# A two-layer batched kernel: another order for batch 0, adapter sums turned by VectorE, and the last batch's parts finished one behind the other

## Chip, cores and metric

One core of one Trainium2 chip. The metric is the device time in microseconds of one execution.

## The reference, cut to what matters

```python
# B, S, D = 8, 256, 1024; rank 16, 32 adapters
sign = (2 * mask - 1)                          # mask[b] is 1024 x 1024, int32
x = x + (x @ W0.T + b0 + (x @ sign) * coeff[b])    # layer 1
A, Bw = lora_A_w[ids[b]], lora_B_w[ids[b]]
x = x + (x @ W1.T + b1 + (x @ A.T) @ Bw.T)         # layer 2
```

Everything is float32. Each factor is split into a high part in the matmul's reduced format (fp32r) and a low part, the rest; three of the four products are summed.

## The kernel before

Layer 1 of a batch is folded into one matrix: W = W0.T + I + coeff x (2 mask - 1). It is made and used in 8 chunks of 128 output columns, so the kernel has 64 chunks n (b = n // 8, c = n % 8). For a chunk VectorE makes W from the mask (`make_w`, L589), ScalarE its high part (`chunk_hi`, L421), VectorE the low part (`chunk_lo`, L596). TensorE multiplies by x (`layer1`, L756 and L758: for each of 8 k one product of 512 columns, x high and low side by side, and one of 256). ScalarE adds the bias and VectorE adds the two halves to y (`half_y` L447, `make_y` L603), then y is split (`y_parts_hi` L454, `y_parts_lo` L607). y is stored transposed, so it serves as the stationary operand of layer 2.

Layer 2 adds, for chunk c, y's chunk times 1024 columns of W1.T + I and 16 columns of adapter A into six PSUM parts (two halves st of the rows, three parts j of the columns; `layer2`, L800 to L802, three products each of some 344 columns). In batch 0 it is four parts of 512 columns (`first_layer2`, L778 to L780) and the adapter has a product of its own (`adapter_h`, L766). After a batch's last chunk the 16 adapter columns h must be turned and multiplied by adapter B and the bias: ScalarE copies them to SBUF (`move_h`, L469), TensorE transposes them (`turn_h`, L811), ScalarE and VectorE split them into `ht` (`h_parts_hi` L476 and L478, `h_parts_lo` L617), and one product per part finishes it (`finish`, L829; batch 0: L820). ScalarE and VectorE move the parts to `zst` in turn (L489, L629), and SP stores them (`store_z`, L286).

Each engine runs its own list, and semaphores tie the lists. Batch 0 also prepares: W0, W1, the adapters and x of batch 0 arrive row by row and are turned on TensorE in units of four 128 x 128 transposes (`turn_unit`, L734), 40 units in all: W0 and W1 16 each, x 4, adapters A and B 2 each. POOL adds the identity to a piece's diagonal block first (`eye_w0` L341, `eye_w1` L347), and splits the bias b1 (L374, L376) and sorts adapter B (L381). ScalarE and VectorE copy or split what was turned (`copy_w0`, `split_hi`, `split_lo` L561; x: L437, L579). The order of all this around the 8 chunks of batch 0 is written in loops over n on each engine. SP issues all large loads in one queue, each waiting for its buffer (`load_mask` with 4 buffers, `load_w0` with 3, `load_w1` with 2). From batch 1 on x is turned by VectorE (`turn_rows`, L566) out of `xraw`, two calls per batch.

At a batch's change TensorE's list is: four of the eight k of the next chunk's layer1, two groups of layer2, the other four k, `turn_h`, four groups, six finishes. After the last chunk there is no layer1: layer2 groups (0,0), (1,0), (0,1), (1,1), `turn_h`, (0,2), (1,2), six finishes.

## Time and profile before

| | us |
|---|---|
| median of 3 runs | 410.96 (410.69 to 412.39) |
| the profiled execution | 411.09 |
| its span, first to last instruction | 409.3 |
| TensorE matmuls busy | 396.6 (97%) |
| VectorE busy | 283.1 (69%) |
| ScalarE busy | 183.8 (45%) |
| POOL busy | 27.4 (7%) |

The runs time a whole execution; the span lies inside it, 1.8 us shorter. Durations are of that one execution. Matmuls are pipelined: two neighbours overlap in the rows, and the distance between starts tells what one costs. PE is TensorE, PEld its weight loads, DVE VectorE, ACT ScalarE, SPq the issues of DMAs on SP.

### The profile page before, as it was taken

The numbers are of one execution on the slowest core, as the hardware profiler recorded it, in microseconds if no ns is written. First come the engines' busy times: TensorE is split into PE (matmuls) and PEld (weight loads), VectorE is DVE, ScalarE is ACT, GpSimd is POOL, SyncE is SP. The second block draws the span as 40 slices with busy tenths as digits, with TensorE's granted clock in tenths as the row PEclk, the third lists the DMA queues.
The fourth block names the chain that finished last, engine by engine and source line by source line (L and its number), as shares of the span: only waits on it lengthen the run. The fifth ranks groups of instructions, "written<-read, shape, count | busy, mean of one in ns | idle before, by whom it ended". The sixth has DMA issues, their size and how long they took to land.

```text
span 409.3 us, 6109 instructions
## 1 busy us (share of the span) xinstructions
PE 396.6 (97%) x2358; PEld 364.1 (89%) x2358; DVE 283.1 (69%) x343; ACT 183.8 (45%) x294; POOL 27.4 (7%) x42
## 2 busy tenths in 40 slices
PE   4899999999999999999999999999999999999995
PEld 3787788899999999999999999999999999999994
DVE  1667978867876688577886679575986679575622
ACT  3565675543444344344444345353444334353322
POOL 2224121000001000010001000010001000000000
PEclk9999999999999999999999999999999999999999
DMA  8999986259531893159531893249731793246002
GB/s 282 267 284 270 272 220 172 73 151 254 150 102 57 200 246 98 58 141 246 166 103 56 200 217 110 75 129 216 200 98 49 197 232 107 88 130 168 0 2 103
DMA packets 93633, 63.33 MB, mean 155 GB/s; under 512 B 3612, under 2 KB 90916, under 8 KB 93605
## 3 DMA queue, kind: packets, MB, share of 16 engines
q1 hardware_dynamic: 93586, 62.95, 58.3%
q8 instruction: 19, 0.31, 0.3%
q14 instruction: 10, 0.07, 0.1%
q10 hardware_dynamic: 18, 0.00, 0.0%
HBM read 51.39 MB, written 8.39 MB: 146 GB/s over the span
## 4 chain that ended last, share of the span: by engine, by line
PE 95%; DMA 2%; SPq 1%; DVE 1%; issue 0%; POOL 0%; ACT 0%; DVEq 0%
PE ps L756 29%; PE ps L758 15%; PE ps L802 13%; PE ps L801 13%; PE ps L800 13%; PE ps L734 4%; DMA w0raw<-in_L_cond_W_dram 2%; PE ps L780 2%; PE ps L778 2%; PE ps L779 2%; PE ps L829 2%; PE ps L766 1%; PE ps L811 0%; DVE wm L589 0%; POOL w0raw L341 0%
## 5 line engine op out<-in xcount | busy, mean ns | idle before, releaser
L756 PE MATMUL ps<-xhl,whi 128*128 128x512 f32 x512 | 184.8, 399 | 0.0
L758 PE MATMUL ps<-xhl,wlo 128*128 128x256 f32 x512 | 143.4, 280 | 0.0
L756 PEld LDWEIGHTS ps<-xhl,whi 128*128 128x128 f32 x512 | 96.5, 188 | 20.0 <-DVE xhl L579 0.4
L800 PE MATMUL ps<-w1hi,yhl 128*128 128x344 f32 (+1 forms) x336 | 108.1, 322 | 0.0
L802 PE MATMUL ps<-w1hi,yhl 128*128 128x344 f32 (+1 forms) x336 | 107.7, 321 | 0.0
L801 PE MATMUL ps<-w1lo,yhl 128*128 128x344 f32 (+1 forms) x336 | 107.6, 320 | 0.0
L596 DVE SCALAR_TENSOR_TENSOR wlo<-wm,cs_minus,whi 128x1024 fp32r<-128x1024 f32 x64 | 81.6, 1274 | 25.3 <-ACT whi L421 25.2
L758 PEld LDWEIGHTS ps<-xhl,wlo 128*128 128x128 f32 x512 | 97.0, 189 | 0.3
L421 ACT ACTIVATE whi<-wm,cs_minus 128x1024 fp32r<-128x1024 f32 x64 | 73.7, 1152 | 43.0 <-DVE wm L589 42.9
L589 DVE SCALAR_TENSOR_TENSOR wm<-wm,cs_twice,w0t 128x1024 f32<-128x1024 int32 x64 | 83.8, 1310 | 10.3 <-ACT w0t L402 8.4
L447 ACT ACTIVATE ysum<-ps,b0col 128x256 f32<-128x256 f32 x64 | 30.3, 474 | 85.5 <-PE ps L758 85.3
L800 PEld LDWEIGHTS ps<-w1hi,yhl 128*128 128x128 f32 x336 | 63.1, 188 | 2.6
L603 DVE TENSOR_TENSOR ysum<-ps,ysum 128x256 f32<-128x256 f32 x64 | 27.1, 424 | 53.1 <-ACT ysum L447 53.1
L801 PEld LDWEIGHTS ps<-w1lo,yhl 128*128 128x128 f32 x336 | 63.2, 188 | 0.0
L802 PEld LDWEIGHTS ps<-w1hi,yhl 128*128 128x128 f32 x336 | 63.1, 188 | 0.0
L454 ACT ACTIVATE yhl<-ysum 128x256 fp32r<-128x256 f32 x64 | 26.7, 417 | 28.6 <-DVE ysum L603 27.5
L566 DVE STREAM_TRANSPOSE xt<-xraw 128x1024 f32<-128x1024 f32 x14 | 31.1, 2220 | 4.2 <-DMA xraw<-in_x_dram 4.2
L607 DVE TENSOR_TENSOR yhl<-ysum,yhl 128x256 fp32r<-128x256 f32 x64 | 27.5, 430 | 1.5 <-ACT yhl L454 1.5
L432 ACT ACTIVATE xhl<-xt 128x1024 fp32r<-128x1024 f32 x14 | 14.9, 1061 | 20.5 <-DVE xt L566 20.5
L356 POOL CAST w1hi<-at 128x128 fp32r<-128x128 f32 x7 | 6.6, 940 | 223.7 <-PE ps L802 223.7
L572 DVE TENSOR_TENSOR xhl<-xt,xhl 128x1024 fp32r<-128x1024 f32 x14 | 17.1, 1221 | 0.2 <-ACT xhl L432 0.2
L734 PE MATMUL ps<-ident,w0raw 128*128 128x128 f32 x64 | 11.3, 313 | 5.7 <-POOL w0raw L341 5.7
(68 smaller groups left out, 217.3 us busy)
## 6 DMA issues: line engine op xcount, KB each, us to landing
wm<-in_mask_Bx4096x_ik_dram SPq DMA_DIRECT2D x64, 512.0 KB, 4.4
xraw<-in_x_dram SPq DMA_DIRECT2D x28, 256.0 KB, 5.8
w0raw<-in_L_cond_W_dram SPq DMA_DIRECT2D x8, 512.0 KB, 7.2
w1raw<-_L_cond_base_weight_dram SPq DMA_DIRECT2D x8, 512.0 KB, 7.4
out_dram<-zst SPq DMA_DIRECT2D x20, 172.0 KB, 2.1
bt<-bhl SPq DMA_DIRECT2D x48, 64.0 KB, 2.3
out_dram<-zst SPq DMA_DIRECT2D x8, 176.0 KB, 2.2
out_dram<-zst SPq DMA_DIRECT2D x8, 164.0 KB, 2.2
```

The lines of the kernel that those rows point to most:

```text
L421: nc.scalar.activation(whi[:, n % WS, :, :], wm[:, n % MS, :].rearrange("p (k o) -> p k o", k=KT), ACT.Identity, bias=cs_minus[:, b:b + 1] ...
L447: nc.scalar.activation(ysum[:, n % 2, :], ps[:, l1_bank(n), S:2 * S], ACT.Identity, bias=b0col[:, n % KT:n % KT + 1]).then_inc(y_half, 1)
L566: nc.vector.transpose(xt[:, :, :].rearrange("p t (n q) -> p n t q", q=Q), xraw[:, :, :].rearrange("p n (i k) -> p n k i", k=KT)[:, :, g * ...
L589: nc.vector.scalar_tensor_tensor(chunk, chunk.bitcast(I32), cs_twice[:, b:b + 1], w0t[:, c, :, :].rearrange("p k o -> p (k o)"), ALU.mult, ...
L596: nc.vector.scalar_tensor_tensor(wlo[:, s, :, :], wm[:, n % MS, :].rearrange("p (k o) -> p k o", k=KT), cs_minus[:, b:b + 1], whi[:, s, :, ...
L607: nc.vector.tensor_tensor(yhl[:, n % 2, S:2 * S], ysum[:, n % 2, :], yhl[:, n % 2, 0:S].bitcast(F32), ALU.subtract).then_inc(y_lo, 1)
L734: op = nc.tensor.transpose(ps[:, bank, m * P:(m + 1) * P], cut[m], ident[:, :])
L756: nc.tensor.matmul(ps[:, bank, :], whi[:, s, k, :], xhl[:, b % 2, k, :], start=(k == 0), stop=False, skip_group_check=True)
L758: op = nc.tensor.matmul(ps[:, bank, 0:S], wlo[:, s, k, :], xhl[:, b % 2, k, 0:S], start=False, stop=(k == KT - 1), skip_group_check=True)
L800: nc.tensor.matmul(dst, hi, w1hi[:, c, cols], start=(c == 0), stop=False, skip_group_check=True)
L801: nc.tensor.matmul(dst, hi, w1lo[:, c, cols], start=False, stop=False, skip_group_check=True)
L802: op = nc.tensor.matmul(dst, lo, w1hi[:, c, cols], start=False, stop=(c == KT - 1), skip_group_check=True)
```

## The change

- SP's loads of batch 0 are written out in a new order: mask 0 ahead of x, W1's pieces 0 and 1 earlier, W0's pieces 4 and 3, 5 and 6 ahead of W1's 3, and so on. W1 has a third buffer (in `xt`, used once), A and B of the adapters have buffers of their own, and the number of loads stays.
- The lists of ScalarE, VectorE, POOL and TensorE for batch 0 are written out. Chunks 0 and 1 are made in halves (`half_make_w`, `half_chunk_hi`, `half_chunk_lo`). layer1(0) comes ahead of W0's piece 1; further on the units stand between pairs of k and between groups of layer 2. `bt` is cleared later, once A has been turned.
- TensorE gets 12 products of zeros (`idle_products`) in front of layer1(0): 5, 2, 2 and 3.
- `move_h` and TensorE's `turn_h` go. VectorE turns the sums straight out of PSUM with four 32 x 64 transposes (`turn_h`), in its list ahead of `h_parts_lo` and `make_y` of the batch's first chunk. Batches 1 to 7 do this.
- Last batch: group (1,2) of chunk 62 is held back until after groups (0,0) and (1,0) of chunk 63; then (0,1) and (0,2), four finishes, (1,1), its finish, (1,2), its finish. The parts are stored in five DMAs, of which the third store takes two parts and the fifth part's is issued by ScalarE.

The rest of the lists for batch 0, not shown here, goes on in the same manner.

```diff
     W0S = 3
-    W1S = 2
+    W1S = 3
...
-             ("w0", 1, 0, 0), ("w0", 1, 1, 1), ("w1", 0, 0, 2), ("w1", 0, 1, 3)]
+             ("w0", 1, 0, 0), ("w0", 1, 1, 1), ("w1", 0, 0, 2), ("w1", 0, 1, 3), ("w0", 2, 0, TB[0]), ("w0", 2, 1, TB[1])]
     for n in range(1, KT):
-        if n + 1 < KT:
+        if 1 < n < KT - 1:
             units += [("w0", n + 1, h, TB[h]) for h in range(2)]
+        if n in (4, 5):
+            units.append(("b", 0, n - 4, TB[1]))
+        units += [("w1", n, h, TB[h]) for h in range(2)]
         if n == 2:
-            units += [("a", 0, 0, TB[1]), ("a", 0, 1, HB)]
-        if n in (3, 4):
-            units.append(("b", 0, n - 3, TB[1]))
-        units += [("w1", n, h, TB[h]) for h in range(2)]
+            units += [("a", 0, 0, HB), ("a", 0, 1, TB[0])]
...
+    LAST = ((0, 0), (1, 0), (0, 1), (0, 2), (1, 1), (1, 2))
+    HELD = ((1, 2),)
...
+        zeros = nc.alloc_sbuf_tensor_at("zeros", [P, HALF], F32R, offset=xt_at)
...
-            sp.dma_start(xrows[:, 0, :], x[0, 0:P, :]).then_inc(rows_in[0], 16)
             load_mask(0)
-            sp.dma_start(xrows[:, 1, :], x[0, P:2 * P, :]).then_inc(rows_in[1], 16)
-            sp.dma_start(b0row[:, :], b0.rearrange("(c p) -> c p", p=P)).then_inc(b0_in, 16)
+            load_rows(0)
+            load_b0()
+            load_rows(1)
             load_w0(1)
             load_mask(1)
             sp.wait_ge(ids_in, 16)
+            load_w1(0)
             names = read_names(range(0, 4))
-            load_w1(0)
             load_w0(2)
-            names += read_names(range(4, NB))
+            load_w1(1)
+            names += read_names(range(4, 8))
             load_mask(2)
-            load_w1(1)
-            load_a(range(0, 2))
+            load_w0(4)
             load_w0(3)
+            load_b1()
+            load_a(range(0, 4))
+            load_w1(2)
             load_mask(3)
-            load_a(range(2, 5))
-            load_w1(2)
-            load_a(range(5, NB))
-            load_w0(4)
-            sp.dma_start(b1raw[:, :], b1.rearrange("(e o) -> e o", e=1)).then_inc(b1_in, 16)
-            for n in range(NS):
...
+            load_a(range(4, 8))
+            load_w0(5)
+            load_w0(6)
+            load_w1(3)
+            load_mask(4)
+            load_w1(4)
+            load_b(range(0, 8))
+            load_mask(5)
+            move_bias()
+            load_w0(7)
+            load_w1(5)
+            load_x(1)
+            load_mask(6)
+            load_w1(6)
+            load_mask(9)
+            load_mask(7)
+            load_mask(8)
+            load_w1(7)
+            load_bt(0)
+            load_mask(11)
+            load_mask(10)
+            for n in range(KT, NS):
                 b, c = divmod(n, KT)
                 if n + 4 < NS:
                     load_mask(n + 4)
...
-            for q in range(6):
-                store_z(NB - 1, q)
+            for t in (0, 1, 3, 5):
+                store_last(t)
...
+            def clear_bt():
+                pool.wait_ge(unit_turned, number["a", 0, 1] + 1)
+                nc.gpsimd.memset(bt[:, :].bitcast(F32), 0.0).then_inc(consts_set, 1)
...
+            bias_parts()
             eye_w0(4)
             eye_w1(3)
+            clear_bt()
             eye_w0(5)
...
+            eye_w1(4)
+            sort_b()
             eye_w0(6)
-            eye_w1(4)
             eye_w0(7)
+            place_a(1)
             eye_w1(5)
+            place_a(2)
             eye_w1(6)
             eye_w1(7)
...
-            def move_h(b):
-                act.wait_ge(h_done, b + 1)
-                if b >= 2:
-                    act.wait_ge(h_turned, b - 1)
-                cut = z_cut(b, 0)[3]
-                nc.scalar.activation(h_row[:, :, :], ps[:, ZB[0][0]:ZB[1][0] + 1, cut],
-                                     ACT.Copy).then_inc(h_moved, 1)
...
+            act.wait_ge(coeff_made, 2)
+            half_chunk_hi(0, 0)
             first_rows_hi(0, 0)
+            half_chunk_hi(0, 1)
             first_rows_hi(0, 1)
-            chunk_hi(0)
             first_rows_hi(1, 0)
             first_rows_hi(1, 1)
+            half_y(0)
             copy_w0(1, 0)
             copy_w0(1, 1)
-            chunk_hi(1)
-            half_y(0)
+            split_hi("w1", 0, 0)
+            half_chunk_hi(1, 0)
+            copy_w0(2, 0)
+            half_chunk_hi(1, 1)
+            copy_w0(2, 1)
+            split_hi("w1", 0, 1)
             y_parts_hi(0)
...
+            for t in (0, 2, 4):
+                move_z(NB - 1, t)
+            cols = z_cut(NB - 1, LAST[4][1])[2]
+            act.wait_ge(z_moved_act, moves_before(NB))
+            act.dma_start(out[NB - 1, P:2 * P, cols], zst[:, 1, cols]).then_inc(z_stored[1], 16)
...
+            def half_make_w(n, g):
+
+                dve.wait_ge(mask_in[n], 16)
+                dve.wait_ge(w0_copied, 2 * n + g + 1)
+                half = wm[:, n, g * HALF:(g + 1) * HALF]
+                op = nc.vector.scalar_tensor_tensor(half, half.bitcast(I32), cs_twice[:, 0:1],
+                                                    w0t[:, n, g * TG:(g + 1) * TG, :].rearrange("p k o -> p (k o)"), ALU.mult, ALU.add)
+                if g == 0:
+                    op.then_inc(first_made, 1)
+                else:
...
+            def turn_h(b):
+
+                dve.wait_ge(h_done, b + 1)
+                if b >= 2:
+                    dve.wait_ge(h_hi, h_hi_before(b))
+                first = z_cut(b, 0)[3].start
+                for a in range(P // Q):
+                    op = nc.vector.transpose(h_rows[:, :, a * Q:(a + 1) * Q],
+                                             ps[a * Q:(a + 1) * Q, ZB[0][0]:ZB[1][0] + 1, first:first + Q])
+                op.then_inc(h_turned, 1)
+
             def h_parts_lo(b):
                 dve.wait_ge(h_hi, h_hi_before(b) + 1)
-                nc.vector.tensor_tensor(ht[32:32 + R, :], ps[0:R, l1_bank(KT * b + 9), 0:S], ht[0:R, :].bitcast(F32),
+                nc.vector.tensor_tensor(ht[32:32 + R, :], h_rows[0:R, :, :].rearrange("r t m -> r (t m)"), ht[0:R, :].bitcast(F32),
...
-            make_w(0)
+            half_make_w(0, 0)
+            half_make_w(0, 1)
+            half_chunk_lo(0, 0)
             first_rows_lo(0, 0)
+            half_chunk_lo(0, 1)
+            first_rows_lo(1, 0)
+            move_b0()
             first_rows_lo(0, 1)
-            chunk_lo(0)
-            first_rows_lo(1, 0)
-            make_w(1)
             first_rows_lo(1, 1)
-            dve.wait_ge(b0_turned, 1)
-            nc.vector.tensor_copy(b0col[:, :], ps[:, L1B, 0:KT]).then_inc(b0_moved, 1)
-            chunk_lo(1)
             make_y(0)
+            half_make_w(1, 0)
+            half_make_w(1, 1)
+            half_chunk_lo(1, 0)
+            split_lo("w1", 0, 0)
+            half_chunk_lo(1, 1)
+            split_lo("w1", 0, 1)
             y_parts_lo(0)
...
+            def idle_products(count):
+
+                for _ in range(count):
+                    nc.tensor.matmul(ps[:, TB[0], :], zeros[:, 0:P], zeros[:, :], start=True, stop=True)
+
+            pe.wait_ge(consts_set, 1)
+            idle_products(5)
             pe.wait_ge(ident_set, 2)
             turn_unit("w0", 0, 0)
             turn_unit("w0", 0, 1)
             pe.wait_ge(coeff_spread, 1)
             nc.tensor.transpose(ps[:, L1B, 0:NB], cs_rows[:, :], ident[0:NB, 0:NB]).then_inc(coeff_turned, 1)
-            for st in range(ST):
-                for g in range(2):
-                    turn_unit("x", st, g)
-            for h in range(2):
-                turn_unit("w0", 1, h)
-            pe.wait_ge(b0_in, 16)
-            pe.wait_ge(coeff_made, 2)
-            nc.tensor.transpose(ps[:, L1B, 0:KT], b0row[:, :], ident[0:KT, 0:KT]).then_inc(b0_turned, 1)
+            idle_products(2)
+            turn_unit("x", 0, 0)
+            turn_unit("x", 0, 1)
+            idle_products(2)
+            turn_b0()
+            turn_unit("x", 1, 0)
+            turn_unit("x", 1, 1)
+            idle_products(3)
             layer1(0, range(0, 8))
+            turn_unit("w0", 1, 0)
+            turn_unit("w0", 1, 1)
...
+            turn_unit("w0", 2, 0)
+            turn_unit("w0", 2, 1)
+            turn_unit("w1", 1, 0)
+            layer1(1, range(0, 2))
+            turn_unit("w1", 1, 1)
+            layer1(1, range(2, 4))
+            layer1(1, range(4, 6))
+            layer1(1, range(6, 8))
+            first_layer2(0, 0, 0)
+            first_layer2(0, 1, 0)
+            first_layer2(0, 0, 1)
+            turn_unit("w0", 3, 0)
+            first_layer2(0, 1, 1)
+            turn_unit("w0", 3, 1)
+            turn_unit("w1", 2, 0)
+            layer1(2, range(0, 2))
...
+            pe.wait_ge(y_lo, NS)
+            layer2(NS - 1, 0, 0)
+            layer2(NS - 1, 1, 0)
+            for st, j in HELD:
+                layer2(NS - 2, st, j)
+            layer2(NS - 1, 0, 1)
+            layer2(NS - 1, 0, 2)
+            for t in range(4):
+                finish(NB - 1, *LAST[t])
+            for t in (4, 5):
+                layer2(NS - 1, *LAST[t])
+                finish(NB - 1, *LAST[t])
```

## Rows read from the trace of the kernel before

**Rows 1.** The page: the chain that ended last, by engine.
```profile
PE 95%; DMA 2%; SPq 1%; DVE 1%; issue 0%; POOL 0%; ACT 0%; DVEq 0%
```

**Rows 2.** Timeline, TensorE, 10 to 24 us: start, us, instruction, idle before.
```profile
10.17 1.97 PE L734 MATMUL ps<-ident,xrows 128*128 128x128 f32 x8 [1.37 <-DMA xrows<-in_x_dram]
...
13.12 1.94 PE L734 MATMUL ps<-ident,w0raw 128*128 128x128 f32 x8 [0.98 <-POOL w0raw L341]
...
16.00 0.63 PE L756 MATMUL ps<-xhl,whi 128*128 128x512 f32 x1
...
16.64 0.58 PE L756 MATMUL ps<-xhl,whi 128*128 128x512 f32 x1
...
19.26 1.03 PE L734 MATMUL ps<-ident,w1raw 128*128 128x128 f32 x8
...
23.13 0.39 PE L756 MATMUL ps<-xhl,whi 128*128 128x512 f32 x1
...
23.48 0.40 PE L756 MATMUL ps<-xhl,whi 128*128 128x512 f32 x1
```

**Rows 3.** Windows: busy us of each engine, granted clock, DMA share, GB/s.
```profile
14.00:18.00 4.00, 3.95 (x15) 2.99 (x15) 1.96 (x3) 2.07 (x3) 1.42 (x2) 1.00 0.78 229
```

**Rows 4.** Timeline, TensorE: the long hole, and the start of layer1(9).
```profile
36.98 0.70 PE L766 MATMUL ps<-yhl,at 128*128 128x512 f32 x2 [0.86 <-issue]
...
83.00 0.40 PE L756 MATMUL ps<-xhl,whi 128*128 128x512 f32 x1
```

**Rows 5.** Timeline, the end: VectorE's three moves, SP's six issues.
```profile
404.12 1.35 DVE L629 COPY zst<-ps 128x344 f32<-128x344 f32 x3 [0.70 <-PE ps L829]
404.43 2.80 SPq L286 DMA_DIRECT2D out_dram<-zst  x6
```

**Rows 6.** Timeline, VectorE and ScalarE, 7 to 18 us.
```profile
7.02 0.15 DVE L636 TENSOR_SCALAR cs_minus<-ps 128x8 f32<-128x8 f32 x1
...
12.18 0.60 ACT L437 ACTIVATE xhl<-ps 128x512 fp32r<-128x512 f32 x1 [0.26 <-PE ps L734]
...
17.00 0.68 DVE L579 TENSOR_TENSOR xhl<-ps,xhl 128x512 fp32r<-128x512 f32 x1
```

**Rows 7.** Timeline, TensorE: one unit and three products, then three products.
```profile
24.53 0.60 PE L734 MATMUL ps<-ident,w1raw 128*128 128x128 f32 x4
...
25.67 0.39 PE L778 MATMUL ps<-w1hi,yhl 128*128 128x512 f32 x1
...
26.37 0.60 PE L734 MATMUL ps<-ident,w1raw 128*128 128x128 f32 x4
```

**Rows 8.** Timeline, POOL: W1's pieces 0 and 3, taken up when landed.
```profile
15.16 0.45 POOL L347 TENSOR_TENSOR w1raw<-w1raw,ident 128x128 f32<-128x128 f32 x1 [2.18 <-DMA w1raw<-_L_cond_base_weight_dram]
...
38.20 0.54 POOL L347 TENSOR_TENSOR w1raw<-w1raw,ident 128x128 f32<-128x128 f32 x1 [4.11 <-DMA w1raw<-_L_cond_base_weight_dram]
```

**Rows 9.** Timeline, 30 to 34 us: POOL's split of b1 beside VectorE.
```profile
30.32 2.37 POOL L376 TENSOR_TENSOR b1lo<-b1raw,b1hi 1x1024 fp32r<-1x1024 f32 x1
...
30.72 3.06 DVE L589 SCALAR_TENSOR_TENSOR wm<-wm,cs_twice,w0t 128x1024 f32<-128x1024 int32 x1 [2.06 <-ACT w0t L402]
```

**Rows 10.** Timeline at the end of batch 1: the adapter sums' way to the finish.
```profile
125.04 0.20 ACT L469 ACTIVATE h_row<-ps 128x32 f32<-128x32 f32 x1 [1.88 <-PE ps L802]
...
126.25 0.38 PE L811 MATMUL ps<-ident,h_row 128*16 128x128 f32 x2
...
126.62 0.31 PE L801 MATMUL ps<-w1lo,yhl 128*128 128x344 f32 x1
126.66 0.38 ACT L476 ACTIVATE ht<-ps 16x256 fp32r<-16x256 f32 x1 [1.43 <-PE ps L811]
...
127.07 0.42 ACT L478 ACTIVATE ht<-ht 16x256 fp32r<-16x256 f32 x1
...
128.35 1.09 PE L829 MATMUL ps<-bt,ht 128*128 128x328 f32 x6
```

**Rows 11.** Groups by line: VectorE's transposes of x; count, busy us, mean ns.
```profile
L566 DVE STREAM_TRANSPOSE xt<-xraw 128x1024 f32<-128x1024 f32 x14 | 31.1, 2220 | 4.2 <-DMA xraw<-in_x_dram 4.2
```

More of the change, by code:

```diff
@@ new lines, in _ @@
+            chunk_lo(3)
+            make_y(2)
+            make_w(4)
+            split_lo("w1", 3, 0)
+            split_lo("w1", 3, 1)
+            y_parts_lo(2)
+            chunk_lo(4)
+            make_y(3)
+            make_w(5)
+            split_lo("b", 0, 0)
+            y_parts_lo(3)
+            split_lo("w1", 4, 0)
+            split_lo("w1", 4, 1)
+            chunk_lo(5)
+            make_y(4)
+            turn_rows(1, 1)
+            split_lo("b", 0, 1)
+            make_w(6)
+            split_lo("w1", 5, 0)
@@ new lines, in _ @@
+            y_parts_lo(4)
+            split_lo("w1", 5, 1)
+            chunk_lo(6)
+            make_y(5)
+            make_w(7)
+            rows_lo(1, 1)
+            y_parts_lo(5)
+            chunk_lo(7)
+            split_lo("w1", 6, 0)
+            make_y(6)
+            make_w(8)
+            split_lo("w1", 6, 1)
+            y_parts_lo(6)
+            turn_rows(1, 0)
+            chunk_lo(8)
+            rows_lo(1, 0)
+            make_y(7)
+            make_w(9)
+            split_lo("w1", 7, 0)
@@ new lines, in _ @@
+            turn_unit("w1", 3, 0)
+            layer1(3, range(0, 2))
+            adapter_h(0)
+            turn_unit("w1", 3, 1)
+            adapter_h(1)
+            layer1(3, range(2, 4))
+            layer1(3, range(4, 6))
+            turn_unit("w0", 5, 0)
+            turn_unit("w0", 5, 1)
+            layer1(3, range(6, 8))
+            first_layer2(2, 0, 0)
+            turn_unit("b", 0, 0)
+            turn_unit("w1", 4, 0)
+            layer1(4, range(0, 2))
+            adapter_h(2)
@@ L888, in _ @@
+            first_layer2(7, 1, 1)
+            first_finish(1, 0)
+            first_finish(1, 1)
+            for n in range(KT + 1, NS):
                 b, c = divmod(n, KT)
```

415 lines of the change are left out of this document (258 added, 157 removed).

## The prediction, made before the changed kernel was run

> **What bounds the kernel now.** I read the page's chain of waits first. It is TensorE's own work for 95% of the span [rows 1], so time is won only where TensorE idles, where it is given less to do, or after its last product. The timeline of TensorE shows three such places. The reader is to look at start times: matmuls overlap, so the distance from one start to the next is the cost, not the duration.
>
> First, the start. The last rows of x are turned at 10.17, the next turning waits for W0's second piece until 13.12, the first products of layer 1 come after it, and the end of layer1(0) is where W1's first transposes start, at 19.26 [rows 2]. Until about 17 us TensorE is slow: one pair of layer1 (512 and 256 columns) starts 0.64 us after the one before at 16.00, and 0.35 us after at 23.13 [rows 2]; that is the 1.2 GHz level against the 2.4 GHz level, although the granted clock of the stretch is recorded as 1.00 [rows 3]. Second, the rest of batch 0, up to the start of layer1(9) at 83.00 [rows 4]. Third, the tail: six stores are issued one behind the other on SP in 2.80 us [rows 5].
>
> **Batch 0, the start.** The change loads the mask second and x third, splits chunk 0 into halves, and puts layer1(0) ahead of both turnings of W0's second piece. x's second half is still the fourth large load, so it can't be there before 10.17 [rows 2]. Ahead of it SP now issues b0 too, a 4 KB load; I cost that at nothing. From 10.17 the chain is: two turnings of x, ScalarE's high parts at 0.60 each, VectorE's low parts at about 0.68 each [rows 6], of which three come after the second x turning (VectorE does halves of x in the order 0,0; 1,0; 0,1; 1,1). Best case, at full clock: turned at 11.1, first low part ready at 12.5, last at 13.9, the second four pairs of layer1(0) then take 4 x 0.35 = 1.4, so it ends at 15.3. Worst case, at half clock: x's first half, third load now, lands at about 8.4 (10.17 less the 1.8 us that half a MiB takes, worked out below); its turnings take 1.97 until 10.4, two idle products at 0.43 until 11.3, x's second turnings until 13.3, then high and low parts until 15.4, and layer1(0) ends near 17. I take 16.3. The idle products (12 of 512 columns) lie in waits: 5 before the first weights, the others while ScalarE and VectorE split x. If that cover were gone they would cost 12 x 0.23 = 2.8 us at full clock.
>
> A rule of the Trainium skill speaks against the low end (page "TensorE: Matmul & The Clock Gate", Part 4: PE-mode transpose): a transpose doesn't count as activity for the clock as a product does. The trace doesn't contradict it: transposes ran at 13.12 and the clock rose only after products had begun [rows 2]. It is a rival below.
>
> **Batch 0, the rest.** The reader can count TensorE's work from layer1(0)'s end to layer1(9)'s start. A unit of four transposes costs 0.44: from 24.53 to 25.67 a unit and three products pass (1.14), from 25.67 to 26.37 three products alone (0.70) [rows 7]. After the change 34 units stand there (w0 of pieces 1 to 7, w1 of all 8, a and b): 15.0. Eight layer1 at 8 x 0.353 = 2.82: 22.5. Thirty-two layer-2 groups at 0.70: 22.2. Eight adapter products at 0.23: 1.9, four finishes: 0.9. Sum 62.5. Now it is 32 units (61.6) in 83.00 - 19.26 = 63.7, so 2.1 is lost today; the one large piece is 0.86 at 36.98 [rows 4]. The changed order loses something else: after layer1(0) ScalarE and VectorE must, in this order, finish y, copy two halves of W0, make both halves of chunk 1, copy W0's third piece and split W1. TensorE has 7 units (3.1 us) to cover this, but the seventh waits for a copy that stands behind five 0.60 us steps on ScalarE; walking the queues gives a hole of some 1.2 us. Everything after it moves together with loads: between W1's piece 0 at 15.16 (3.5 MiB loaded) and piece 3 at 38.20 (10 MiB) the queue brought 6.5 MiB in 23.0 us, 3.54 us each [rows 8]. In the new order of SP, W1's piece 3 stands at 9.0 MiB, hence 34.7; TensorE reaches it at 16.3 + 18.2 + 1.2 = 35.7. All of lora B is at 10.5 MiB, hence 40.0, and must still be sorted; TensorE wants it at about 41.4. x of batch 1 is at 13 MiB (11.5 now), hence 48.8, and VectorE stands before its turn_rows, with splits for TensorE behind it, from about 48. These are close, so I add 0.8 for small holes. Batch 0 would then end at 16.3 + 62.5 + 1.2 + 0.8 = 80.8, against 83.0: **2.2 us less**. Bounds: 15.3 + 62.5 + 0.8 = 78.6 (4.4 less), and 17.0 + 62.5 + 3.5 = 83.0 (nothing).
>
> The parts of b1 matter here too: at 30.72 a VectorE step took 3.06, while POOL ran its 2.37 us subtraction on one row until 32.69 [rows 9], so it may have stood for up to 1.97. TensorE's one long hole today follows it. The subtraction is still made at about that time, so the collision is likely again. If it hits a step that TensorE awaits, that is 2.0 us at most; it is within the upper bound of 3.5.
>
> **Adapter sums on VectorE, batches 1 to 6.** TensorE loses two transposes per batch. From 126.25 to 126.62 two transposes and one product pass; a product of layer 2 costs 0.16 (344 of 512 columns, at 0.70 for three), so the pair costs 0.21 [rows 10]. Six batches: **1.3 us less**. What comes in is four 32 x 64 transposes out of the banks of sums. No row shows this; from below, VectorE's read of an 8-column bank takes 0.15 [rows 6], from above the 128 x 1024 transpose takes 2.22 [rows 11]. Its length scales to 0.14 for 64 elements, plus such a start: I take 0.2 each, 0.8 in all, as the size is near the small row. They are hidden: today the sums are ready at 125.04, the high part starts at 126.66, and the finish at 128.35 [rows 10]. The high part and its copy pass from 126.66 to 127.49, 0.83, and without the pair TensorE is at the finish at 128.1, so the four may take 128.1 - 125.0 - 0.9 = 2.2 us before TensorE waits. Behind them on VectorE stand h's low part and make_y, and the latter is due only when layer1 ends at 126.25 and ScalarE has added the bias; ScalarE in fact reaches that sooner, as h's parts come earlier. The copies into bt stay where they are.
>
> **The last batch.** A group of three products costs 0.48 here. Today four groups, the two transposes and six finishes follow the adapter sum: 1.92 + 0.21 + 0.96 = 3.1. After the change the sum is reached one group (the held one) earlier; then come three groups (1.44), against 0.8 + 0.83 + gaps of 0.2 for the sums' way to the finish, so a stall of 0.4; four finishes (0.64), and twice a group and a finish (1.28): 3.8 in all. TensorE so ends 0.2 later than now. The last move takes a third of 1.35 and follows it at once, while now it waits for the move before it (three from 404.12, ending at 405.47 [rows 5]): it ends at about 405.5 either way. But its store is then issued at once, by an SP that has nothing else left. Today the sixth issue starts at 404.43 + 2.80 - 0.47 = 406.8 [rows 5]. So the end comes **1.3 us earlier**; bounds 0.7 (VectorE's transposes at 0.35 each) and 1.7 (no stall). My 0.2 each lets each of the four begin as the one before it drains. The Trainium skill has a rule against the change here ("VectorE: DVE Perf Modes", section Two Vector instructions with no wait between them): an instruction whose input starts in another quadrant of partitions than that of the one before is held until all before it have finished. By it the four would not overlap, and the end would come 1.1 instead of 1.3 us earlier.
>
> **Sum.** 2.2 + 1.3 + 1.3 = 4.8. The profiled execution took 411.09 with a span of 409.3; I expect a span of 404.5 and an execution of 406.3. The median of the runs shown is 410.96, 0.13 below the profiled one: 406.2.
>
> **Rivals.**
> (a) Batch 0 goes nearly without holes, and TensorE is fast from x's turning on: 4.4 + 1.3 + 1.3 = 7.0 less, 404.0. For it: the start is a chain of small waits that all shrink. Against: the loads that it needs come at the same rate. Chance 0.22.
> (b) Loads and queues bind: w1, b and x(1) land a little later than worked out, VectorE stands before turn_rows with the splits behind it, and batch 0 gives nothing: 2.6 less, 408.4. For it: every due time above lies within 1.5 us of its landing. Chance 0.16.
> (c) Transposes don't warm TensorE, so all up to layer1(0) is at half clock and three of its pairs too: layer1(0) ends at 17.0 + 3 x 0.29 = 17.9, 1.6 later than I take, so 3.2 less in all: 407.8. For it: the late rise in the trace; against: the idle products are products. The page named above has this rule. Chance 0.12.
> (d) The other side: VectorE's transposes read PSUM slowly. With s each, a batch stalls 4s - 2.2 and the end 4s - 0.8 more than worked out; the gain of 4.8 is gone, and 2.05 more, where 6(4s - 2.2) + (4s - 0.8) is over 6.85, from s = 0.75. At 1.0 it is 14 us against 4.8, some 420. At 2.22, the long row, it would be far more. Against: 64 elements are a sixteenth of that row. Chance 0.03.
> (e) The change doesn't do what it says, since the stores bind: the last one waits for something other than SP's issues, so the tail stays: 3.5 less, 407.5. Little speaks for it: 406.8 plus the 2.5 us to the end of the span is what one store needs. Chance 0.05, left in the range.
>
> **How the numbers follow.** A difference of 0.5%, 2.05 us, is about what a measurement can tell. My forecast (405.1 to 407.4) has 0.42. It, (a), (c) and (e) are faster by more; of (b) two thirds is too, the rest is within 0.5%. Faster 0.91, same 0.06, slower 0.03. The range takes (a) down to 403.4 and (b) up to 408.5, and leaves out (d), the lower end of (a) and the upper of (b).
>
> **What would show it.** TensorE's pair spacing at 0.35 from about 13 us; layer1(0) ending near 16.3; layer1(9) starting near 80.8; no TensorE transposes at the batch boundaries, with four VectorE transposes of 0.2 there; a hole of 0.4 ahead of the last finishes; the last store issued within 0.1 of the last move. A start of layer1(9) at 83 or later, or a TensorE hole ahead of the finishes of batches 1 to 6, would make it wrong.

## The result, and the profile after

| | before | after |
|---|---|---|
| median of 6 runs each | 411.42 us (410.69 to 416.54) | 409.10 us (407.21 to 412.30) |
| ratio, with its 95% interval | | 0.9935 (0.9908 to 0.9963) |
| the profiled execution | 411.09 | 409.28 |
| its span | 409.3 | 407.5 |

The kernel is faster, by 1.8 us between the two profiled executions and by 2.3 us between the medians; 4.8 us were predicted, so the time lies above the range (403.4 to 408.5). Two later measurements (runs 5 and 12) gave 408.67 against 412.09 (0.9916, 0.9886 to 0.9945) and 408.91 against 412.46 (0.9915, 0.9887 to 0.9943). One kernel's executions lie up to 5 us apart (407.21 to 412.30 here). The ratios leave out five slow executions, which the medians still hold: one of 654 us in each of runs 5 and 10, one of 1385 us in run 6, and two of 417 us in run 8.

The page after, its chain of waits by engine, against 95% for PE before [rows 1]:

```profile
PE 90%; DMA 5%; SPq 3%; issue 1%; DVE 1%; ACT 0%
```

DMA rose from 2 to 5%, and SP's issues (SPq) from 1 to 3%. From the chain of waits between 26 and 57 us these are the transfers and the steps behind them (start, us, what; the pieces left out are TensorE's work and issues on SP):

```profile
26.58 4.61 DMA araw<-in_L_cond_lora_A_w_dram
31.32 0.63 PE ps L919 x4
...
44.33 8.97 DMA xraw<-in_x_dram
53.36 2.06 issue
55.42 1.07 DVE bhl L670
```

**Batch 0.** TensorE's timeline:

```profile
8.45 1.97 PE L919 MATMUL ps<-ident,xrows 128*128 128x128 f32 x8 [0.39 <-DMA xrows<-in_x_dram]
...
14.03 0.47 PE L946 MATMUL ps<-xhl,whi 128*128 128x512 f32 x1
...
14.46 0.40 PE L946 MATMUL ps<-xhl,whi 128*128 128x512 f32 x1
...
14.81 0.40 PE L946 MATMUL ps<-xhl,whi 128*128 128x512 f32 x1
...
16.93 1.05 PE L919 MATMUL ps<-ident,w0raw 128*128 128x128 f32 x8
...
20.32 0.66 PE L919 MATMUL ps<-ident,w1raw 128*128 128x128 f32 x4 [0.57 <-ACT w0t L470]
...
31.32 0.63 PE L919 MATMUL ps<-ident,araw 128*128 128x128 f32 x4 [0.85 <-DMA araw<-in_L_cond_lora_A_w_dram]
...
56.53 0.66 PE L919 MATMUL ps<-ident,w1raw 128*128 128x128 f32 x4 [1.33 <-DVE bhl L670]
...
83.23 0.39 PE L946 MATMUL ps<-xhl,whi 128*128 128x512 f32 x1
```

Pairs of layer1(0) start 0.35 apart, the 2.4 GHz level, where they were 0.64 apart at 16.00 before [rows 2]; layer1(0) ends at 16.93 instead of 19.26, 2.3 earlier. And layer1(9) starts at 83.23, where it was 83.00 [rows 4]: all of it was given back. In the rows stand 0.57 before W1's piece 1, 0.85 before lora A and 1.33 before a unit that waits for VectorE's split of lora B. By the starts they cost 0.75, 1.0 and 1.5, and smaller ones another 0.5. Up to 83.23, 16.93 and the prediction's 62.5 of work leave 3.8 us of holes. POOL's and VectorE's timelines say when the loads came:

```profile
35.51 0.46 POOL L405 TENSOR_TENSOR w1raw<-w1raw,ident 128x128 f32<-128x128 f32 x1 [2.83 <-DMA w1raw<-_L_cond_base_weight_dram]
...
40.69 1.24 POOL L419 COPY bsort<-braw 128x1024 f32<-128x1024 f32 x1 [1.20 <-DMA braw<-in_L_cond_lora_B_w_dram]
```

```profile
53.32 2.20 DVE L677 STREAM_TRANSPOSE xt<-xraw 128x1024 f32<-128x1024 f32 x1 [2.37 <-DMA xraw<-in_x_dram]
55.42 1.06 DVE L670 TENSOR_TENSOR bhl<-ps,bhl 128x512 fp32r<-128x512 f32 x1
```

W1's piece 3 and lora B came 0.8 and 0.7 later than worked out, x of batch 1 4.5 later. VectorE stood 2.37 us for it, then turned it for 2.20, with the split that TensorE wanted behind it.

One thing more shows in the queue of loads. After the issue of mask 2, at 13.68, SP issued nothing until 18.01: W0's piece 4 needs a buffer that comes free only when W0's piece 1 is turned, and the change puts that turning behind layer1(0), at 16.93. SP's waits and the DMA engines' load (the columns of the window are the stretch, busy us of PE, PEld, DVE, ACT, POOL, granted clock, DMA share, GB/s):

```profile
SPq L276 <- PE ps L919: 4.7, 3, 3.7
```

```profile
17.00:19.00 2.00, 2.00 (x20) 2.00 (x20) 1.16 (x3) 1.87 (x4) 0.46 (x1) 1.00 0.70 177
```

In the kernel before, the same two microseconds had a share of 1.19 and 323 GB/s, though SP stood for buffers there too, at other times (3.7 us at the longest). The change thus moved work on TensorE, and with it the time at which some loads could be issued.

**A batch's change, and the end.** VectorE and ScalarE at the end of batch 1, then the last batch:

```profile
125.19 1.02 DVE L762 STREAM_TRANSPOSE h_rows<-ps 32x64 f32<-32x64 f32 x4 [0.57 <-PE ps L997]
126.24 0.42 ACT L548 ACTIVATE ht<-h_rows 16x256 fp32r<-16x256 f32 x1 [2.93 <-DVE h_rows L762]
...
128.29 1.09 PE L1018 MATMUL ps<-bt,ht 128*128 128x328 f32 x6
...
399.87 1.01 DVE L762 STREAM_TRANSPOSE h_rows<-ps 32x64 f32<-32x64 f32 x4 [1.47 <-PE ps L997]
...
401.88 0.85 PE L1018 MATMUL ps<-bt,ht 128*128 128x328 f32 x4 [0.62 <-ACT ht L550]
...
402.78 2.14 SPq L336 DMA_DIRECT2D out_dram<-zst  x4
...
404.03 0.53 DVE L780 COPY zst<-ps 128x352 f32<-128x352 f32 x1 [0.65 <-PE ps L1018]
```

TensorE has no wait before the finish at 128.29, and from it to batch 6's at 358.78 there are 46.10 us per batch, against 46.31 before (128.35 to 359.89). From the batch-1 finish to the end of the span it is 279.2 against 280.9, 1.7 less: five times 0.21, and 0.7 from the tail. The first stretch adds up too: 0.23 more up to layer1(9), 0.29 less from there to the finish at 128.29, 1.7 less after: 1.8.

### The profile page after: what moved, and what is told of

The parts are those of the page before. It is cut to its first block, busy times and chain, and to the rows that moved or that the text cites. A ratio compares the mean times of both kernels' runs of the same rounds, so it can differ in the third digit from the quotient of the medians.

```text
span 407.5 us, 6136 instructions
## 1 busy us (share of the span) xinstructions
PE 397.8 (98%) x2356; PEld 365.3 (90%) x2356; DVE 290.6 (71%) x375; ACT 183.2 (45%) x289; POOL 26.5 (7%) x43
## 4 chain that ended last, share of the span: by engine, by line
PE 90%; DMA 5%; SPq 3%; issue 1%; DVE 1%; ACT 0%
PE ps L946 28%; PE ps L948 14%; PE ps L997 13%; PE ps L996 13%; PE ps L995 13%; PE ps L919 3%; DMA xraw<-in_x_dram 2%; PE ps L1018 2%; DMA xrows<-in_x_dram 2%; SPq L292 1%; PE ps L975 1%; PE ps L974 1%; PE ps L973 1%; DMA araw<-in_L_cond_lora_A_w_dram 1%; SPq L261 0%
## 5 line engine op out<-in xcount | busy, mean ns | idle before, releaser
L707 DVE SCALAR_TENSOR_TENSOR wlo<-wm,cs_minus,whi 128x1024 fp32r<-128x1024 f32 x62 | 80.0, 1291 | 20.7 <-ACT whi L487 20.7
L487 ACT ACTIVATE whi<-wm,cs_minus 128x1024 fp32r<-128x1024 f32 x62 | 71.5, 1153 | 39.7 <-DVE wm L700 39.7
L700 DVE SCALAR_TENSOR_TENSOR wm<-wm,cs_twice,w0t 128x1024 f32<-128x1024 int32 x62 | 80.1, 1291 | 3.9 <-DMA wm<-in_mask_Bx4096x_ik_dram 2.8
L429 POOL CAST w1hi<-at 128x128 fp32r<-128x128 f32 x7 | 5.3, 752 | 223.8 <-PE ps L997 223.8
L973 PE MATMUL ps<-w1hi,yhl 128*128 128x512 f32 x32 | 13.3, 415 | 0.0
```

Source lines behind the costliest of these rows:

```text
L487: nc.scalar.activation(whi[:, n % WS, :, :], wm[:, n % MS, :].rearrange("p (k o) -> p k o", k=KT), ACT.Identity, bias=cs_minus[:, b:b + 1] ...
L700: nc.vector.scalar_tensor_tensor(chunk, chunk.bitcast(I32), cs_twice[:, b:b + 1], w0t[:, c, :, :].rearrange("p k o -> p (k o)"), ALU.mult, ...
L707: nc.vector.scalar_tensor_tensor(wlo[:, s, :, :], wm[:, n % MS, :].rearrange("p (k o) -> p k o", k=KT), cs_minus[:, b:b + 1], whi[:, s, :, ...
```

## The experiments

Theory A: the queue of large loads sets batch 0, so whatever TensorE saves ahead of them comes back as holes; the sums' turning is hidden. Rival B: the holes come from the order of the engines' lists and from VectorE steps stretched beside POOL.

**1. VectorE's turning alone**, in the kernel before.

```diff
-                    move_h(b - 1)          # ScalarE
...
-                        turn_h(b - 1)      # TensorE
...
+                    turn_h(b - 1)          # VectorE, ahead of h_parts_lo
```

> The kernel before with one part of the change alone: VectorE turns the adapter sums, everything else as before. Theory A (the steady parts paid as worked out, batch 0 paid nothing): 1.3 to 1.5 us less than before, TensorE's transposes at L811 gone, batch 0 still ends near 83.0, a start-to-start distance of batches of about 46.1 instead of 46.3. Theory B (the gain of the change came from batch 0 and VectorE's turning paid nothing): the time of before within 0.4 us, since a new wait of 0.2 stands ahead of the finishes.

Measured: 411.37 against 411.76, ratio 0.9985 (0.9964 to 1.0005): 0.4 less, which is B's number and not A's 1.3 to 1.5. The steady part is as A has it, 46.10 per batch. But its batch-1 finish came at 129.53, 1.2 later than before's 128.35, though TensorE was at the 2.4 GHz level early. TensorE's timeline shows where it went:

```profile
41.02 0.63 PE L736 MATMUL ps<-ident,bsort 128*128 128x128 f32 x4 [1.71 <-POOL bsort L381]
...
52.75 0.63 PE L736 MATMUL ps<-ident,w1raw 128*128 128x128 f32 x4 [1.83 <-POOL w1raw L347]
```

POOL in its turn waited there for the loads of lora B (1.19) and of a piece of W1 (10.87). So the old order waits for loads as well when its start is quick (layer1(0) ended at 18.14, layer1(9) started at 84.39), and the profiled execution of before was one of its good ones: its time, 411.09, is under each of the medians of before from six and more runs (411.42, 411.76, 412.09, 412.46).

**2. The changed kernel with the old batch 0.** The turning and the tail are new, the lists of batch 0 on all engines as before.

```diff
-    W1S = 3
+    W1S = 2
...
-            half_make_w(0, 0)
-            half_make_w(0, 1)
+            make_w(0)
...
-            idle_products(3)
             layer1(0, range(0, 8))
```

> The changed kernel with the batch 0 of before on every engine: VectorE's turning and the new end remain. Theory A: 2.4 to 2.8 us less than before, so as fast as the changed kernel within 0.5 us, since the new order of batch 0 moved its holes and closed none. Theory B: at most 1 us less than before, because batch 0 brought the rest.

Measured: 411.02, ratio 0.9983 (0.9959 to 1.0007), span 408.6. This speaks against A as I had put it: A wanted 2.4 to 2.8 us less than before, and it is 0.7 less, which is what B had (at most 1). Against the changed kernel's ratios of 0.9935, 0.9916 and 0.9915, taken in other measurements, the new batch 0 is worth 2.0 to 2.8 us. Profiles show less. The adapter sums (six times 0.21) and the tail (0.6, run 11) make 1.9 us in them; taken from the 2.7 to 3.5 that the changed kernel's ratios stand for, 0.8 to 1.6 are left for batch 0. And layer1(9) starts at 83.00, 83.52 and 84.39 in the three profiles with the old order, at 82.8 to 83.7 in the six with the changed kernel's lists of batch 0 (the changed kernel three times, runs 8, 11 and 13). So the new batch 0 does gain something over many executions, between about 1 and 3 us; how much, and by what, the runs leave open. That it gave nothing holds for the profiled pair alone.

**3. No idle products.**

```diff
-            pe.wait_ge(consts_set, 1)
-            idle_products(5)
...
-            idle_products(2)
...
-            idle_products(2)
...
-            idle_products(3)
```

> The changed kernel without the 12 products of zeros. If they are what brought TensorE to 2.4 GHz before layer1(0): its first pairs start 0.64 apart, layer1(0) ends near 18 instead of 16.9, and the later holes that wait for loads (1.0 us at A, 1.5 us at B's second half) shrink, so that the time stays within 0.5 us of the changed kernel. If TensorE alone set the time of batch 0, it would be 1 us slower. If the turnings alone warm TensorE, nothing moves at all.

Measured: 409.98, ratio 0.9964 (0.9940 to 0.9989). TensorE's timeline:

```profile
11.24 1.98 PE L919 MATMUL ps<-ident,xrows 128*128 128x128 f32 x8
13.87 0.77 PE L946 MATMUL ps<-xhl,whi 128*128 128x512 f32 x1 [0.65 <-DVE xhl L690]
...
14.65 0.63 PE L946 MATMUL ps<-xhl,whi 128*128 128x512 f32 x1
...
15.29 0.63 PE L946 MATMUL ps<-xhl,whi 128*128 128x512 f32 x1
...
18.47 0.40 PE L946 MATMUL ps<-xhl,whi 128*128 128x512 f32 x1
```

Seven pairs stand about 0.64 apart, the 1.2 GHz level, and layer1(0) ends at 18.82, 1.9 later; with the zero products all of layer1(0) ran at 0.35 in the changed kernel. But run 1, which has no zero products either, had turnings only in front of layer1(0), and there the 2.4 GHz level came before the first pair:

```profile
12.50 1.13 PE L736 MATMUL ps<-ident,w0raw 128*128 128x128 f32 x8 [1.26 <-POOL w0raw L341]
...
13.72 0.50 PE L758 MATMUL ps<-xhl,whi 128*128 128x512 f32 x1
...
14.18 0.39 PE L758 MATMUL ps<-xhl,whi 128*128 128x512 f32 x1
```

Eight turnings took 1.13 there and 1.94 in the kernel before, whose order of turnings is the same. So turnings alone brought the level once and not at other times, and the zero products are one way to have it early, not the only one. The batch-1 finish is 0.8 later than in the changed kernel's first profile (129.07 against 128.29): over half of the 1.9 us vanished in the holes behind, as A has it. By time the run is 1.2 to 2.0 us slower than the changed kernel (0.9964 against 0.9935, 0.9916 and 0.9915), where I expected at most 0.5.

**4. The split of lora B ahead of the turning of x(1)** on VectorE.

```diff
-            turn_rows(1, 1)
             split_lo("b", 0, 1)
+            turn_rows(1, 1)
```

> The changed kernel, with one exchange in VectorE's list: the low part of adapter B's second half comes ahead of the first turning of x(1) instead of behind it. The loads stay as they are. If VectorE standing before x(1), which landed at 53.3, is what held TensorE for 1.5 us until 56.5: the split runs near 52.5, this hole goes, and batch 0 ends 1 to 1.5 us earlier, unless the next piece of W1 or chunk 6 is then late, which would show as a new hole at W1's piece 6 or chunk_lo(6). If the hole belongs to the load of B or to POOL, it stays.

**5. The changed kernel again**, beside runs 6, 7 and 8.

> The changed kernel itself, once more, as the measure for the three beside it: a ratio of 0.993 to 0.995 to the kernel before, and in its trace the two holes of TensorE that wait for lora A (0.8 to 1.2 us near 31) and for B's second half behind VectorE's wait for x(1) (about 1.3 us near 56).

Measured: 409.47, ratio 0.9936 (0.9915 to 0.9957), for 4, and 408.67, 0.9916 (0.9886 to 0.9945), for 5, a little faster than the 0.993 to 0.995 expected, with 0.81 before lora A and 0.93 near 56 us. In 4 the hole near 56 us is gone, and 0.59 stands at 59.76 and 0.49 at 29.13; lora A's is 1.19, which the changed kernel also shows without this edit (1.13 in run 12). Nothing gained.

**6. Lighter loads.** Half of masks 4 to 11 and half of W0's and W1's pieces 3 to 7 are not loaded, so the kernel computes on stale halves; all instructions of the engines stay.

```diff
+                ks = KT // 2 if n < 12 and n >= MS else KT
+                cols = D // 2 if c >= W0S else D
+                ms = KT // 2 if c >= W1S else KT
```

> The changed kernel, with half the bytes of masks 4 to 11 and of the pieces 3 to 7 of W0 and W1: the other halves are left out, so 4.5 MiB less are loaded in batch 0, while every engine's list, wait and operation stays. Theory A (what is left in batch 0's holes after layer1(0) are loads that land late): lora A lands 1.5 us or more earlier and x(1) several us, both holes go, layer1(9) starts between 79.5 and 80.8, and the time is 2 to 3 us below the changed kernel. Theory C (the queues of ScalarE, VectorE and POOL are as tight as the loads): TensorE's holes change their places, but less than 1 us is gained.

Measured: 407.70, ratio 0.9869 (0.9833 to 0.9906), span 405.7; layer1(9) at 81.46 although layer1(0) ended 0.4 later than in 5. That is 1.0 us below run 5 by the medians and 1.9 by the ratios, where A had 2 to 3, and layer1(9) is later than A's 79.5 to 80.8; C had less than 1. From layer1(0)'s end to layer1(9) it takes 64.0 us, against 65.9 to 66.3 in the changed kernel's three profiles, so the holes lost 1.9 to 2.3 us. Two windows, 17 to 33 and 33 to 57 us, of this kernel and of the changed one (run 12), with the columns as above:

```profile
17.00:33.00 16.00, 15.07 (x102) 13.31 (x101) 14.15 (x17) 10.90 (x20) 7.77 (x7) 1.00 0.86 242
33.00:57.00 24.00, 24.00 (x146) 20.69 (x146) 19.74 (x24) 15.55 (x26) 6.77 (x12) 1.00 0.62 157
```

```profile
17.00:33.00 16.00, 14.29 (x95) 12.45 (x94) 12.15 (x17) 11.06 (x20) 6.61 (x6) 1.00 1.00 281
33.00:57.00 24.00, 23.10 (x142) 19.69 (x141) 17.67 (x21) 13.97 (x25) 9.11 (x13) 1.00 0.98 244
```

In the changed kernel the DMA share is near 1 on the average of either window, though not at every moment (0.70 from 17 to 19 us, above, and 0.42 from 39 to 41 in the profile after); with fewer bytes TensorE is busy throughout the second window. Of the waits 0.60 is left before W1's piece 1 (ScalarE's chain of copies) and 0.34 before lora A, there behind VectorE and not behind a load. This shows that over half of batch 0's holes come from the loads. It doesn't show that the loads ran as fast as they can: SP's waits for buffers also hold them back, and no run takes these away.

**7. x(1) loaded earlier, lora A turned later.**

```diff
+            load_x(1)
             load_w0(7)
             load_w1(5)
-            load_x(1)
...
-            turn_unit("a", 0, 0)
             layer1(2, range(4, 6))
             layer1(2, range(6, 8))
+            turn_unit("a", 0, 0)
```

> The changed kernel with two exchanges: SP loads x(1) ahead of W0's piece 7 and W1's piece 5 (1 MiB earlier, so 3.5 to 4 us sooner), and TensorE turns lora A's first half behind the last four k of layer1(2) instead of ahead of them (1.4 us later). Theory A: the hole near 56 goes and the one near 31 shrinks to under 0.4, 1 to 2 us are won against the changed kernel, if W1's piece 5 (needed near 53) doesn't land late instead, which would show as a hole before its turning. Theory C: under 0.5 us won.

Measured: 408.77, ratio 0.9911 (0.9877 to 0.9945), layer1(9) at 83.07 against 82.97 in 5: nothing won. Lora A's unit still waits 0.71 instead of under 0.4, now for VectorE's split of W1 (`w1lo`). The wait for x(1) is all but gone (0.23 on VectorE), and W1's piece, now behind it in the queue, makes one as long:

```profile
54.57 0.63 PE L919 MATMUL ps<-ident,w1raw 128*128 128x128 f32 x4 [1.38 <-POOL w1raw L405]
```

**8. Four more VectorE transposes** ahead of the four, into a spare tile.

```diff
+                for a in range(P // Q):
+                    nc.vector.transpose(h_spare[:, a, :, :],
+                                        ps[a * Q:(a + 1) * Q, ZB[0][0]:ZB[1][0] + 1, 0:Q])
```

> The changed kernel, where VectorE makes four more transposes of the same size, out of the same banks into a spare place, ahead of the four of the adapter sums. As worked out, four cost about 1.0 us (0.25 each). If the cover at the batch boundaries is 2.2 us, eight (2.0) still leave TensorE without a hole there and batches stay 46.1 apart, while in the last batch the hole ahead of the finishes grows from 0.6 to 1.6: 1.0 us slower in all. If the cover is smaller or VectorE's list is what binds (make_w and chunk_lo come 1 us later in each first chunk), every boundary costs up to 1 us: 7 us slower.

Measured: 411.96, ratio 0.9977 (0.9951 to 1.0002), span 409.0. At the end:

```profile
400.38 1.01 DVE L762 STREAM_TRANSPOSE h_spare<-ps 32x64 f32<-32x64 f32 x4 [1.47 <-PE ps L1001]
401.40 1.01 DVE L766 STREAM_TRANSPOSE h_rows<-ps 32x64 f32<-32x64 f32 x4
...
403.41 0.86 PE L1022 MATMUL ps<-bt,ht 128*128 128x328 f32 x4 [1.64 <-ACT ht L551]
```

In the batches the finishes start at 127.89, 174.03, 220.12, 267.04, 313.13 and 359.27, none after a wait, and so 46.14, 46.09, 46.92, 46.09 and 46.14 apart. Four distances are those of the changed kernel within 0.03. The one long one comes from a load of x that landed late, in this one batch, over 20 us after the transposes:

```profile
240.91 2.22 DVE L678 STREAM_TRANSPOSE xt<-xraw 128x1024 f32<-128x1024 f32 x1 [3.08 <-DMA xraw<-in_x_dram]
```

```profile
244.35 0.50 PE L950 MATMUL ps<-xhl,whi 128*128 128x512 f32 x1 [0.54 <-DVE wlo L708]
```

So a microsecond more on VectorE costs at most 0.03 in a batch and a whole 1.02 at the end. The cover in a batch is at least the 2.03 that the eight take, as the prediction's 2.2 had it.

**9. b1's parts early:** loaded by ScalarE's queue, split on POOL behind W0's first piece.

```diff
-            load_b1()
...
+            act.dma_start(b1raw[:, :], b1.rearrange("(e o) -> e o", e=1)).then_inc(b1_in, 16)
...
             eye_w0(0)
+            bias_parts()
...
             eye_w1(2)
-            bias_parts()
```

> The changed kernel, with b1 loaded by ScalarE's queue at the start and POOL's two steps on it made right behind W0's first piece (from about 4.7 us), so that nothing of POOL's stands beside VectorE's make_w(3) at 30 us. Theory (loads set batch 0): VectorE's step at 30 us goes back from 2.1 to 1.28 us, but lora A lands at about 31.3 as before and the hole before its unit stays within 0.3 of 0.8; layer1(9) starts at 82.6 to 83.0 and the ratio to the kernel before stays within 0.002 of the changed kernel's in this call. Rival (VectorE's stretched steps set it): layer1(9) starts 0.8 or more earlier, about 82.1, and the time is 0.8 less than the changed kernel's.

**10. The three mends together:** b1 early, both units of lora A behind layer1(2), and the order of 4.

> All three mends of the holes together: b1 early as in the run above, both units of lora A behind all of layer1(2), and VectorE splitting b's second half ahead of the turning of x(1). Theory (load rate binds, holes only trade places): the holes before lora A's and before the unit near 56 us go, part of them comes back before W1's pieces further on; layer1(9) starts at 82.0 to 82.8, 0.3 to 0.8 us better than the changed kernel. Rival (the lists' order is at fault, not the rate): both holes vanish with nothing in their place, layer1(9) starts at 81.0 to 81.3, 1.7 us or more better.

**12. The changed kernel a third time**, beside runs 9, 10 and 11.

> The changed kernel itself once more, so that the three runs beside it are compared on one chip in one call. Expected 408.7 to 409.1, ratio to the kernel before 0.991 to 0.994.

Measured: 409.33 for 9 (ratio 0.9921, 0.9894 to 0.9948), 408.84 for 10 (0.9906, 0.9881 to 0.9930), 408.91 for 12. VectorE's and TensorE's timelines of 9:

```profile
7.33 2.51 DVE L716 SCALAR_TENSOR_TENSOR wm<-wm,cs_twice,w0t 128x512 f32<-128x512 int32 x2
...
30.31 1.28 DVE L700 SCALAR_TENSOR_TENSOR wm<-wm,cs_twice,w0t 128x1024 f32<-128x1024 int32 x1 [2.86 <-DMA wm<-in_mask_Bx4096x_ik_dram]
```

```profile
31.37 0.63 PE L919 MATMUL ps<-ident,araw 128*128 128x128 f32 x4 [0.87 <-DMA araw<-in_L_cond_lora_A_w_dram]
```

The stretched step is back at 1.28 (2.16 in the profile after), the stretch went with POOL's subtraction to the step at 7.33 (1.41 in the changed kernel), and the hole before lora A stayed at 0.87. So the collision is real and was not on the path: this half of B falls. layer1(9), at 83.42, was even later than expected by A, which had 82.6 to 83.0. In 10 both holes are gone, and smaller ones took their place (0.40 at 28.47, 0.59 at 58.24, others of 0.2 to 0.3); layer1(9) is at 82.71 against 82.82 in 12. I expected A to leave 0.3 to 0.8 of gain, and it left 0.1 (0.1 to 0.5 if counted from layer1(0)'s end), which no measurement here tells from nothing; the other half of B, that the lists' order alone is at fault, had 1.7 or more. No version tried that computes the whole result beats the changed kernel. None gives SP a buffer earlier in the new order, by a fourth one for W0 or W0's piece 1 turned ahead of layer1(0): that cause stays untested.

**11. The old tail** in the changed kernel.

```diff
-    HELD = ((1, 2),)
+    HELD = ()
...
-            for t in (0, 1, 3, 5):
-                store_last(t)
+            for q in range(6):
+                store_z(NB - 1, q)
...
```

> The changed kernel with the last batch ordered as before (six finishes in a row, no group held back, six stores on SP one behind the other); batch 0 and VectorE's turning of the sums are the changed kernel's. It prices the tail by itself. Theory from the two profiles (last move's end to the span's end 2.94 against 3.83 us): 0.7 to 1.3 us slower than the changed kernel. My prediction's sum had 1.3. Rival (the stores bind, the tail gives nothing): the same time as the changed kernel, and the last store of SP starts no later than the last move's end.

Measured: 410.38, ratio 0.9941 (0.9919 to 0.9962), 1.5 above run 12 by the medians. Of the 1.4 between the two profiled executions 0.8 is batch 0 by chance (layer1(9) at 83.64 with the same lists); from the batch-1 finish to the end it takes 279.8 against 279.2, so the tail is worth 0.6, a little less than the 0.7 to 1.3 expected.

**13. Half of the last stores' bytes:** each of the last batch's five stores writes only the first half of its columns.

```diff
+                cols = slice(cols.start, (cols.start + cols.stop) // 2)
```

> The changed kernel, in which each of the last batch's five stores carries only the first half of its columns (half of the last batch's output is not written); moves, waits and the number of issues are the same. Theory (the bytes of the last stores bind the end: 1.05 MB at some 370 GB/s, one store behind the other): the span ends 2.4 to 2.6 us after VectorE's last move ends instead of 2.9 to 3.0, and 0.3 to 0.5 us less from the batch-1 finish to the end. Rival (the last store's own latency binds, as my sum had it): 2.9 to 3.0 stays.

Measured: 408.16, ratio 0.9908 (0.9885 to 0.9931). The span ends 2.27 us after the last move's end (404.50 + 0.53, span 407.3), and from the batch-1 finish to the end it takes 278.5; in the profile after these are 2.94 and 279.2. Both fell by 0.7, more than the 0.3 to 0.5 expected. Windows at the end, of the kernel before, after, and this one:

```profile
406.00:407.00 1.00, 0.00 (x0) 0.00 (x0) 0.00 (x0) 0.00 (x0) 0.00 (x0) 1.00 0.99 354
407.00:408.00 1.00, 0.00 (x0) 0.00 (x0) 0.00 (x0) 0.00 (x0) 0.00 (x0) 1.00 0.97 352
```

```profile
404.00:405.00 1.00, 0.00 (x0) 0.00 (x0) 0.53 (x1) 0.00 (x0) 0.00 (x0) 1.00 0.98 361
405.00:406.00 1.00, 0.00 (x0) 0.00 (x0) 0.00 (x0) 0.00 (x0) 0.00 (x0) 1.00 0.99 375
```

```profile
405.00:406.00 1.00, 0.00 (x0) 0.00 (x0) 0.03 (x1) 0.00 (x0) 0.00 (x0) 1.00 0.83 287
```

With full stores the DMA engines are busy 97 to 99% at 352 to 375 GB/s once they have begun: the last batch is 1.05 MB, so 2.8 to 3.0 us, whoever issues it. Halved, the store lands earlier though nothing else changed. The stores' bytes bind the end, not only their issues. The profiles agree: from the first store's issue to the end of the span it takes 4.9 us in the kernel before (404.43 to 409.3), 4.7 in the changed kernel (402.78 to 407.5) and 4.8 with the old tail (403.67 to 408.5), whatever the order of the issues, and 4.05 here (403.25 to 407.3). The run halves the last store itself together with those in front of it, so it doesn't tell their shares apart.

## Why the prediction was wrong in size, step by step

- **The start** held within its bounds: 16.93 where I took 16.3. x turned at half clock (1.87 and 1.97 for eight), as in my worst case; the products then ran at full clock, so (c) didn't come. Without the idle products it would have: run 3 has seven pairs at 0.64. The rule of the Trainium skill ("TensorE: Matmul & The Clock Gate", Part 4: PE-mode transpose) on which (c) leans, that transposes don't bring the full clock, fits run 3 but not run 1, where turnings alone came down from 1.95 to 1.13 us for eight and the first pair already ran at the 2.4 GHz level; the measurement decides, and the rule doesn't hold for these turnings as it stands.
- **"I add 0.8 for small holes" is the step that failed.** With the 1.2 for the chain of copies I had 2.0; the trace has 3.8, and the six profiles with these lists have 3.4 to 4.3. The chain was sized high (a wait of 0.57, a start 0.75 late). Most of the rest is loads (run 6), and there the step that failed is the one rate, 3.54 us per MiB, carried over from the old order to every load. In the new order W1's piece 0 was taken up at 14.64, and from there piece 3 (5.5 MiB on) came at 3.8 us per MiB and x(1) (9.5 MiB on) at 4.1. Lora A, which bound first, I never costed; but at 3.54 it would have landed at 29.3, a microsecond before TensorE wanted it, and it landed at 31.3, so the rate is what would have hidden it. x(1) was the large miss: W1's piece 5 was taken up at 48.76 and x(1), 1 MiB behind it, at 53.32, 4.6 us later. VectorE stood for it with a split for TensorE behind it, which the prediction had seen and called "close". Rival (b), at 0.16, is what happened to batch 0 in the profiled pair: the 2.2 us of the forecast were -0.2. Over many executions batch 0 did gain something (run 2), but its end, forecast at 80.8, was at 82.8 to 83.7 in all six profiles. Runs 4, 7 and 10 moved the order of compute, run 7 that of a load too, and the holes traded places; only fewer bytes closed them. Why the rate was lower in the new order, SP's waits for buffers or the kinds of loads, is not shown.
- **Adapter sums: right.** 0.21 per batch to the hundredth. The transposes took 0.25 each, not 0.2, and were hidden, with another four hidden as well in run 8. The held rule of the Trainium skill ("VectorE: DVE Perf Modes", Two Vector instructions with no wait between them) agrees: four take 1.01, with no overlap, while the estimate of 0.2 let them overlap.
- **The last batch: 1.3 predicted, 0.7 and 0.6 measured.** The stall is 0.62 instead of 0.4 (four transposes 0.25 each), and the last store, issued at once as said, lands 2.94 after the last move where I had 2.5, the latency of a store that stood alone. I gave (e) 0.05; its mechanism, that something other than SP's issues holds the last store, is half true: the bytes do. The longer stall (0.2) and the longer landing (0.4) are the 0.6 that is missing. What the tail still gains comes from the first store's being issued earlier.
- **The medians** fell more (2.3 to 3.6) than the profiled pair (1.8), since before's profiled execution was a good one. A sum made against one execution carries that execution's luck: here about 1 us. Even so the largest of these falls is 1.2 short of the 4.8.

## What to carry to other kernels

Where loads set a stretch, reordering the compute in it may only move the holes, as in runs 4, 7 and 10. Sum the bytes up to each due time, for every load on the path and not only those that bound before, and don't carry one rate from the old order to the new: look at the DMA share in short windows, and at which compute step frees the buffer that the queue waits for. Price a change at one place by what binds next there. At the end of this kernel the time from the first store's issue to the end hardly changed (4.7 to 4.9 us), so the time of the first store counts as much as that of the last.

## What was unexpected in the hardware

- A VectorE step that reads two SBUF tensors took 2.16 us instead of 1.28 while POOL ran a 2.36 us subtraction on one row; moving the subtraction moved the stretch (2.51 instead of 1.41). The Trainium skill ("GPSIMD Engine Reference", Specifications) says that the two share SBUF interfaces, with contention for instructions with two SBUF inputs; run 9 agrees.
- The same turnings in the same order ran at different levels in two executions: the eight of W0's piece 1 took 1.94 us in the kernel before and 1.13 in run 1, whose TensorE list is the same up to there.
- TensorE's halved speed (pairs 0.64 apart, turnings of eight in 1.97) stands beside a granted clock recorded as 1.00 [rows 3], so the spacing has to be read, not that column.
